# Gate products moved into the image ahead, written over the transposed rows (a vision-transformer layer in float32 on one core)

## The reference

```python
x = layernorm(h)                              # "a" in the kernel
normed = (x - mu) / sqrt(var + EPS) * ln_gamma + ln_beta
q, k, v = split(normed @ W_qkv.T, 3)          # 8 heads of 32
gate = sigmoid(to_heads(x @ W_gate.T + b_gate))
scores = einsum('bhid,bhjd->bhij', q, k) * D ** (-0.5)
attn = softmax(scores)
out = einsum('bhij,bhid->bhjd', attn, v) * gate
h = h + x + out @ W_final.T + b_final
```

## Time and profile before

| | us |
|---|---|
| median of 3 runs | 1819.79 |
| lowest, highest | 1818.34, 1821.87 |
| the profiled execution, its own time | 1824.39 |
| its span, first to last instruction | 1822.6 |
| TensorE busy | 1631.2 (90%) |
| VectorE busy | 1201.0 (66%) |
| ScalarE busy | 943.0 (52%) |
| GpSimdE busy | 307.8 (17%) |
| mean granted TensorE clock | 0.967 of full |

### The profile page before, as it was taken

How to read it: one execution, slowest core, us unless ns; L and a number is a source line. 1 busy time by engine, 2 the same in 40 slices (tenths; PEclk the granted TensorE clock), 3 DMA queues, 4 the chain that set the end, 5 groups by cost and what they waited for, 6 DMA issues and landing times.

```text
span 1822.6 us, 29454 instructions
## 1 busy us (share of the span) xinstructions
PE 1631.2 (90%) x11124; PEld 1125.0 (62%) x11124; DVE 1201.0 (66%) x1904; ACT 943.0 (52%) x1560; POOL 307.8 (17%) x231
## 2 busy tenths in 40 slices
PE   8796999999999999999999999998885707999998
PEld 6463556556646665665657456645443506999998
DVE  2376686868777776777677767776666496444443
ACT  0465655756575657567565756575663331222222
POOL 0202000200200020002001000200000081555554
PEclk9798999999999999999999999999999858999999
DMA  4313235242604251342325141603330462666663
GB/s 162 87 53 69 43 94 132 57 99 64 144 19 111 68 147 23 106 117 81 87 67 131 42 110 53 162 5 89 80 83 20 118 163 90 199 202 204 208 198 129
DMA packets 121218, 187.57 MB, mean 103 GB/s; under 512 B 11883, under 2 KB 86265, under 8 KB 120956
## 3 DMA queue, kind: packets, MB, share of 16 engines
q1 hardware_dynamic: 104652, 120.42, 26.7%
q0 software_dynamic: 16000, 63.98, 10.9%
q10 hardware_dynamic: 432, 1.31, 0.2%
HBM read 84.98 MB, written 51.38 MB: 75 GB/s over the span
## 4 chain that ended last, share of the span: by engine, by line
PE 68%; DVE 18%; issue 7%; ACT 5%; DMA 1%; SPq 1%; POOL 0%; POOLq 0%; DVEq 0%; ACTq 0%
PE ps L509 12%; PE ps L752 11%; PE ps L523 11%; PE ps L476 8%; DVE nmax L1066 6%; ACT pr L854 3%; PE ps L740 3%; PE ps L559 3%; PE ps L536 3%; PE ps L497 3%; PE ps L580 2%; PE ps L582 2%; PE ps L581 2%; PE ps L543 1%; PE ps L450 1%
## 5 line engine op out<-in xcount | busy, mean ns | idle before, releaser
L1066 DVE TENSOR_REDUCE nmax<-ps 128x1 f32<-128x1024 f32 x512 | 623.7, 1221 | 216.7 <-PE ps L509 209.8
L854 ACT ACTIVATE pr<-ps,nmax 128x1024 f32<-128x1024 f32 x512 | 570.7, 1115 | 287.1 <-DVE nmax L1066 282.2
L509 PE MATMUL ps<-st 96*128 96x512 f32 x1024 | 399.6, 474 | 70.5 <-ACT pr L854 60.8
L509 PEld LDWEIGHTS ps<-st 96*128 96x128 f32 x1024 | 168.2, 191 | 266.5 <-ACT pr L854 128.6
L523 PE MATMUL ps<-pr,vs 128*32 128x256 f32 x4096 | 271.7, 386 | 11.5 <-DVE vs L957 11.5
L752 PE MATMUL ps<-wd,hg 128*128 x1728 | 224.9, 287 | 0.0
L752 PEld LDWEIGHTS ps<-wd,hg 128*128 128x128 f32 x1728 | 212.2, 192 | 0.0
L523 PEld LDWEIGHTS ps<-pr,vs 128*32 128x32 f32 x4096 | 108.8, 109 | 153.4 <-issue 70.4
L890 ACT ACTIVATE hg<-ps 128x512 fp32r<-128x512 f32 x144 | 78.6, 596 | 239.6 <-PE ps L740 234.8
L476 PE MATMUL ps<-wp,xt 128*128 128x256 f32 x672 | 172.8, 378 | 0.0
L823 ACT ACTIVATE ht<-ps,bf 128x512 f32<-128x512 f32 x128 | 88.3, 690 | 129.8 <-PE ps L582 129.8
(11 more groups left out here) (129 smaller groups left out, 1885.6 us busy)
## 6 DMA issues: line engine op xcount, KB each, us to landing
st<-qk SPq DMA_DIRECT2D x192, 256.0 KB, 5.1
xt<-x_in SPq DMA_DIRECT2D x58, 384.0 KB, 3.1
token_rows<-staged_b SPq DMA_DIRECT2D x64, 256.0 KB, 4.1
token_rows<-staged_a SPq DMA_DIRECT2D x64, 256.0 KB, 4.1
token_rows<-hres POOLq DMA_DIRECT2D x8, 1024.0 KB, 5.2
wd_raw<-w_down SPq DMA_DIRECT2D x64, 128.0 KB, 3.0
pr<-x_in SPq DMA_DIRECT2D x6, 384.0 KB, 9.0
rows<-token_rows,slot_from POOLq DMA_INDIRECT x72
```

The costliest lines, as they stand in the source:

```text
L509: last = mm(ps[:, 2 * (k % SR) + j, :], stq[:, hh, i * P:(i + 1) * P], stk[:, hh, j * 512:(j + 1) * 512], start=True, stop=True)
L854: actv(pr[:, k % PR, :], ps[:, 2 * (k % SR):2 * (k % SR) + 2, :].rearrange("p a n -> p (a n)"), ACT.Exp, bias=nmax[:, k % 16:k % 16 + 1], ...
L1066: V.reduce_max(nmax[:, k % 16:k % 16 + 1], ps[:, 2 * (k % SR):2 * (k % SR) + 2, :].rearrange("p a n -> p (a n)"), AX_X, negate=True).then_ ...
```

## The change

- `at` and `gate` become one tensor `ga` with two buffers that alternate by image. The transposes of `a` are written into the buffer of their image, the gate products read it, and the tanh writes its result over the half that the products have read.
- All four gate products (eight matmuls) of image b + 1 stand in the second half of image b, at steps 43 to 46 and 48 to 51. The four tanh follow at 46, 47, 51 and 52. Those of image 0 stand between its steps 31 and 32.
- The transposes move from steps 39 to 46 to steps 35 to 42. VectorE reads the four of `a` (`turned_a`), in steps 37, 38, 41 and 42; ScalarE keeps the four of `n`.
- The query and key products move from 49 to 59 with gaps to 53 to 60 without. The low parts follow two steps behind each pair, as before, which now is at 56, 58, 60 and 62. The value products stay at 61 and 63.
- At the start of an image nothing is left between `final` and score 0; the products of steps 0 and 2 now wait for the additions of `final`'s result.

```diff
@@ tensors @@
-        at = tensor(sa, "at", [P, DC, TOKENS])
+        ga = tensor(sa, "ga", [P, 2, DC, TOKENS])
-        gate = tensor(sa, "gate", [P, DC, TOKENS])
...
@@ the semaphore tr_read becomes trn_read and tra_read @@
...
@@ step tables @@
-        GATE_AT = {G_STEPS + 3 + m: divmod(m, 2) for m in range(4)}
-        TURN_AT = {G_STEPS + 7 + j: j for j in range(8)}
-        QK0_AT = {G_STEPS + 17 + 3 * j + c: (j, c) for j in range(4) for c in range(2)}
+        TURN_AT = {G_STEPS + 3 + j: j for j in range(8)}
+        GATE_AT = {G_STEPS + 11 + 5 * hf + 2 * c2 + c: (hf, c2, c) for hf in range(2) for c2 in range(2) for c in range(DC)}
+        TANH_AT = {G_STEPS + 14 + 5 * hf + c2: (hf, c2) for hf in range(2) for c2 in range(2)}
+        QK0_AT = {G_STEPS + 21 + 2 * j + c: (j, c) for j in range(4) for c in range(2)}
@@ TensorE: turn, gates, final @@
                 if j >= 2:
-                    wait(pe, "tr_read", b * 8 + j - 1)
+                    wait(pe, ("tra_read", "trn_read")[w // 2], b * 4 + (j - 2) // 4 * 2 + j % 2 + 1)
...
-            def gates(b, c2, hf, c):
-
-                last = mm(spare(hf), wg[:, c, c2 * P:(c2 + 1) * P],
-                          at[:, c, hf * HALF:(hf + 1) * HALF], start=(c == 0), stop=(c == DC - 1))
+            def gates(b, hf, c2, c):
+
+                if c == 0 and c2 == 0 and hf == 0:
+                    wait(pe, "tra_read", b * 4 + 4)
+                if c == 0 and hf == 1:
+                    wait(pe, "g_tanh", b * 4 + c2 + 1)
+                last = mm(spare(c2), wg[:, c, c2 * P:(c2 + 1) * P],
+                          ga[:, b % 2, c, hf * HALF:(hf + 1) * HALF], start=(c == 0), stop=(c == DC - 1))
...
-                    elif isinstance(b, int) and b == IMAGES - 1:
-                        wait(pe, "g_tanh", b * 4 + 3 + j)
+                    elif b == IMAGES - 1:
+                        wait(pe, "lg_done", b * 2)
...
@@ TensorE: image @@
                 values(b, 1, 1)
                 if before:
                     final(b - 1)
-                for j in range(2):
-                    if before:
-                        wait(pe, "fin_h", b * 4 - 1 + j)
-                    else:
-                        wait(pe, "v_read", b * 4 + 3 + j)
-                    for c in range(DC):
-                        gates(b, 0, j, c)
                 for k in range(STEPS):
                     if k == G_STEPS:
...
+                        if not before:
+                            for hf in range(2):
+                                for c2 in range(2):
+                                    for c in range(DC):
+                                        gates(b, hf, c2, c)
...
                         if j < 2 and c == 0:
-                            wait(pe, "g_tanh", b * 4 + 1 + j)
+                            if before:
+                                wait(pe, "fin_h", b * 4 - 1 + j)
+                            else:
+                                wait(pe, "v_read", b * 4 + 3 + j)
                         project(b, 1, j, c)
...
-                    if k in GATE_AT:
-                        hf, c = GATE_AT[k]
-                        if before and hf == 0 and c == 0:
-                            wait(pe, "lg_done", b * 2)
-                        gates(b, 1, hf, c)
                     if after and k in TURN_AT:
-                        if TURN_AT[k] < 2:
-                            wait(pe, "g_tanh", b * 4 + 3 + TURN_AT[k])
+                        if TURN_AT[k] == 0:
+                            if before:
+                                wait(pe, "lg_done", b * 2)
+                            else:
+                                wait(pe, "g_tanh", b * 4 + 4)
                         turn(b + 1, TURN_AT[k])
+                    if after and k in GATE_AT:
+                        gates(b + 1, *GATE_AT[k])
                     if after and k in QK0_AT:
                         j, c = QK0_AT[k]
-                        if j == 0 and c == 0:
-                            wait(pe, "tr_read", b * 8 + 16)
+                        if j < 2 and c == 0:
+                            wait(pe, "g_tanh", b * 4 + 7 + j)
                         project(b + 1, 0, j, c)
@@ ScalarE: turned keeps the nt half, gated_tanh by half of the tokens @@
-                if w < 2:
-                    actv(nt[:, w, hf * HALF:(hf + 1) * HALF], spare(j), ACT.Identity,
-                         bias=beta[:, w:w + 1], scale=gamma[:, w:w + 1]).then_inc(S["tr_read"], 1)
-                else:
-                    actv(at[:, w - 2, hf * HALF:(hf + 1) * HALF], spare(j), ACT.Identity).then_inc(S["tr_read"], 1)
+                actv(nt[:, w, hf * HALF:(hf + 1) * HALF], spare(j), ACT.Identity,
+                     bias=beta[:, w:w + 1], scale=gamma[:, w:w + 1]).then_inc(S["trn_read"], 1)
...
-            def gated_tanh(b, c, hf):
+            def gated_tanh(b, hf, c):
...
-                wait(act, "g_mm", b * 4 + 2 * c + hf + 1)
-                actv(gate[:, c, hf * HALF:(hf + 1) * HALF], spare(hf), ACT.Tanh,
+                wait(act, "g_mm", b * 4 + 2 * hf + 2)
+                actv(ga[:, b % 2, c, hf * HALF:(hf + 1) * HALF], spare(c), ACT.Tanh,
...
-                    if after and k in TURN_AT:
+                    if after and k in TURN_AT and TURN_AT[k] % 4 < 2:
                         turned(b + 1, TURN_AT[k])
-                    if k in GATE_AT and GATE_AT[k][1] == 1:
-                        gated_tanh(b, 1, GATE_AT[k][0])
+                    if after and k in TANH_AT:
+                        gated_tanh(b + 1, *TANH_AT[k])
...
@@ VectorE @@
+            def turned_a(b, j):
+                hf, w = j // 4, j % 4 - 2
+                wait(dve, "tr_mm", b * 8 + j + 1)
+                V.tensor_copy(ga[:, b % 2, w, hf * HALF:(hf + 1) * HALF], spare(j)).then_inc(S["tra_read"], 1)
...
-                wait(dve, "g_tanh", b * 4 + 2 * (g + 1))
+                wait(dve, "g_tanh", b * 4 + 4)
...
                     if k in LOW1_AT:
                         low(b, 1, LOW1_AT[k])
+                    if after and k in TURN_AT and TURN_AT[k] % 4 >= 2:
+                        turned_a(b + 1, TURN_AT[k])
```

More of the change, by code:

```diff
@@ L179, in vit_layer_kernel @@
                      "stats1 stats3 var1 var3 eps1 eps3 rstd1 rstd3 pow_ready "
-                     "a_ready n_ready xn_ready tr_mm tr_read h_sum ha_ready qk_mm qk_hi qk_lo v_mm v_read "
+                     "a_ready n_ready xn_ready tr_mm trn_read tra_read h_sum ha_ready qk_mm qk_hi qk_lo v_mm v_read "
                      "g_mm g_tanh stack00 stack01 stack02 stack03 stack10 stack11 stack12 stack13 score_mm max_done exp_done rinv_done vs_ready "
@@ L203, in vit_layer_kernel @@
         posr = nt
-        posw2 = at[:, 0, 0:DC * D].rearrange("p (c d) -> p c d", c=DC)
-        posbias = at[:, 1, 0:2 * D].rearrange("p (a d) -> p a d", a=2)
+        posw2 = ga[:, 0, 0, 0:DC * D].rearrange("p (c d) -> p c d", c=DC)
+        posbias = ga[:, 0, 1, 0:2 * D].rearrange("p (a d) -> p a d", a=2)
         x_first = pr[:, 2:7].rearrange("p a n -> p (a n)")[:, 0:(TILES - 2) * KC * P].rearrange(
@@ L558, in final @@
                         for c in range(DC):
-                            last = mm(spare(j)[:, t * D:(t + 1) * D], gate[:, c, (2 * j + t) * P:(2 * j + t + 1) * P],
+                            last = mm(spare(j)[:, t * D:(t + 1) * D], ga[:, b % 2, c, (2 * j + t) * P:(2 * j + t + 1) * P],
                                       wfin[:, c, :], start=(c == 0), stop=(c == DC - 1), skip_group_check=True)
@@ L622, in front_start @@
                     turn(b, j)
-                wait(pe, "tr_read", b * 8 + 8)
+                wait(pe, "trn_read", b * 4 + 4)
+                wait(pe, "tra_read", b * 4 + 4)
                 for j in range(4):
@@ L823, in router @@
                         actv(ht[:, k, :], spare(bank), ACT.Gelu, bias=bf1[:, k:k + 1]).then_inc(S["ff_act"], 1)
-            for j in range(8):
+            for j in (0, 1, 4, 5):
                 turned(0, j)
@@ L836, in image @@
                     valued(b, 1, h)
[L837 to L840, removed]
                 for k in range(STEPS):
+                    if k == G_STEPS and not before:
+                        for hf in range(2):
+                            for c2 in range(2):
+                                gated_tanh(b, hf, c2)
                     if k == G_STEPS and before:
@@ L961, in gated @@
                 wait(dve, "pv_mm", b * 16 + 8 * (g + 1))
-                wait(dve, "g_tanh", b * 4 + 2 * (g + 1))
+                wait(dve, "g_tanh", b * 4 + 4)
                 for j in range(2):
-                    piece = gate[:, g, j * 512:(j + 1) * 512]
+                    piece = ga[:, b % 2, g, j * 512:(j + 1) * 512]
                     V.scalar_tensor_tensor(piece, piece, 1.0, ps[:, O_BANK + j, :], ALU.add, ALU.mult
@@ L1032, in _ @@
             norm_2(0, 0, False)
+            for j in (2, 3, 6, 7):
+                turned_a(0, j)
             for j in range(4):
```

## The result

The changed kernel takes 1890.83 us (median of 4 runs, 1889.0 to 1891.93), the kernel before beside it 1820.83. The ratio is 1.0371, 95% interval 1.0349 to 1.0393: 70 us slower. The forecast was slower at 1868 with a range to 1884; the sign and the place are right, the size is too small.

A forecast was written before the change was run, and what follows sets the result against it. TensorE held 68% of the chain of waits, but VectorE's statistics covered the start. Seven images gave 42.7, seven boundaries 6.3, ends -0.5: +48.5 us on the median 1819.79, so 1868; range 1843 to 1884.

The forecast's parts named there:

- Gate products out of the start: Image boundary: removing 3.04 us of matmuls gains nothing, since VectorE's statistics hold step 0's maximum; TensorE idles 3.6 us.
- The last steps: Steps 56 to 63: odd-step pieces wait for even-step low parts, costing 5.2 us an image.
- the replay: Steps 56 to 63 timed from score 56: last value product starts 18.18 us behind it, where it was 12.96.
- The middle: Second half of an image: added gate matmuls, earlier transposes and reads moved to VectorE together cost 0.9 us an image.
- The chain through step 43: Step 43's gate product waits for VectorE's copy in step 42; score 44 comes at 4.60, 1.25 us late.
- The upper bound: Added gate matmuls in the second half: eight records take 3.4 us, so at most 4 x 0.86 = 3.4 us.
- The clock: Gap at the image boundary: the granted clock falls behind it, costing 0.9 us a boundary, bounds 0 and 1.33.
- My reading of the earlier trace: Third image, steps 34 to 38: the clock fell behind a stretch with little TensorE work, costing 1.33 us.
- The ends: Images 0 and 7 and the kernel's start: together -0.5 us.
- The rival in which the clock falls everywhere: Clock falls at the boundary and in each new wait of steps 57 to 63; 71 more, 1890 us; chance 0.06.
- Rivals of slack: Slack takes the waits of steps 57 to 63, leaving 1827 to 1832 us; chance 0.12.
- a shorter start: Step 0's maximum comes with its score, saving 3.04 us at each of seven boundaries; 1799 us; chance 0.07.

The follow-up runs named there:

- e3_cover: The changed kernel with four unread gate-size matmuls put back between the final projection and score 0 of images 1 to 7; 1889.24 us.
- e2_before_even_low: The kernel before with only the next image's query and key products moved to steps 53 to 60, as in the changed kernel; 1863.76 us.
- e5_third_copy: The changed kernel with step 43's gate product waiting for VectorE's third copy and step 45's channel half for the fourth; 1882.17 us.
- e1_odd_low: The changed kernel with the next image's query and key products one step earlier, at 52 to 59, low parts on odd steps; 1860.07 us.
- e9_before_odd_low: The kernel before with the next image's query and key products at steps 52 to 59 without gaps, low parts on odd steps; 1838.36 us.

## Why the prediction was right or wrong, point by point

- *Gate products out of the start are worth nothing.* Right, and shown by putting their work back (e3_cover). The idle time of TensorE was 3.98, I had 3.6.
- *The last steps.* Right in mechanism, step by step: 5.12, 4.70, 6.04 between the even scores where the replay had 5.00, 4.60, 5.93. The term came out at 5.6 us an image without the clock (4.54 in 56 to 63, 1.1 behind it, e2_before_even_low), against 5.2. Each wait was some 0.1 us longer than my constants. 7 x 0.4 = 3 us.
- *The middle.* Mis-sized: 0.9 taken, 1.60 measured (42 to 46 +1.37, 46 to 52 +0.65, 52 to 56 -0.47, 38 to 42 +0.05). The chain through step 43 had 4.60 for two steps and took 4.70 (355.11 to 359.81), but I let the emptier steps behind it win back more than they did. 7 x 0.7 = 5 us. (The upper bound took 3.4 us for eight records, for which the earlier trace rows has 3.60; the term of 0.9 doesn't hang on it.)
- *The clock.* The step that failed most. I took 0.9 us at one place an image. At the start it was 1.04. A second place, the stretch behind the waits of the last steps, I had put into a rival with a chance of 0.06. There the clock fell in every second image and the boundary took 21.55 instead of 19.97: 1.58 us, or 0.8 on the mean. The term is then 1.84 instead of 0.9: 7 x 0.94 = 7 us. That the waits cause this fall is not shown: e2_before_even_low and e5_third_copy have the same waits in 56 to 63 and took 19.97 at every boundary. A third place, 34 to 38, where the clock fell in each image, I had not in the sum at all; it hides in the difference, since the order there is quicker without a fall (6.95 for 7.18). My reading of the earlier trace rows, too, was off: in the 15 us ahead of that fall TensorE was idle once, for 1.18 us, and the second image has the same idle time without a fall.
- *The ends.* I had -0.5. The start gave -2.5 (the first exponential at 77.76 for 80.23), but the last image, emptied of gate products, lost 2.65 between its first and last exponential, nearly all of it at 34 to 42 with a low clock, and 3.3 came behind its last exponential. Together +3.5, 4 us more than forecast. I had read the last image as a gain. The 3.3 is not the change's: behind the last exponential e1_odd_low and e5_third_copy, with the same code there as the changed kernel, took 432 us, the kernel before 433 and the changed kernel 436.
- The four add up to 19 us, which is what lies between the 48.5 of the sum and the 67.5 measured. The rival in which the clock falls everywhere gave 1890, near the measured time, but its prices were not those: it had 4 us of clock an image, and 1.84 were paid. It hit the sum with a wrong split.
- *Rivals of slack and of a shorter start.* Both out: e2_before_even_low pays the full wait, and VectorE has no idle time in front of the maximum of step 0.
- The Trainium skill's rule (TensorE: Matmul & The Clock Gate, HAM oscillation) speaks of idle gaps that throttle the engine again. The trace agrees: the gap of 3.98 us was followed by a granted clock of 0.51, and the same place without the gap kept 1.00. It held for the start. Of the shorter waits in the last steps it held in four of the seven images of the changed kernel and in none of e2_before_even_low, so it says where to ask and not what the answer is; I should have asked it of each idle time that my own replay made.

## What to carry to other kernels

Before work is moved out of a place, ask what else ends there: TensorE was busy for the whole boundary, yet the next step hung on VectorE's statistics, and only both edits together shortened it. In an order written out by hand, put a waiter two steps behind its producer or on the step whose scores come late; one table shifted by one step was worth 30 us. And look at each idle time that a change opens on TensorE twice, once as waiting and once as clock, also in the stretch that follows and in an image that merely loses work; the second price may be due, may be absent, and may move when something else is edited.

## What the runs showed of the hardware

Less work on TensorE could make a stretch longer. Steps 46 to 51 of e9_before_odd_low, five of the six with nothing but scores and weighing, took 11.67 us with the clock at its lower level, more than the 10.68 of the kernel before with two products more in them. The last image shows that it need not: there such steps took 10.03, with the clock at 1.00. Removing one fall of the clock could move it: e3_cover took 1.04 us away at the start and paid 1.14 at 34 to 38. One fall with 3.4 us at the lower level cost from 0.4 us (34 to 38 of the changed kernel, 7.38 for 6.95) to 1.58 us (the boundary, where TensorE is busy nearly throughout).
